# Attention scores of a unit's first query tile computed with the key tile stationary, copied out of PSUM and transposed back

## The reference, cut to what matters

```python
xn = layernorm(x)                                  # x: 2 x 512 x 512, f32
q = rope((xn @ wq).reshape(B, S, 32, 128))         # 32 query heads
k = rope((xn @ wk).reshape(B, S, 8, 128))          # 8 key heads, 4 query heads share one
v = (xn @ wv).reshape(B, S, 8, 128)
scores = einsum('bqhgd,bshd->bhgqs', qg, k) / sqrt(128)
allowed = (j <= i) & (j > i - 128)                 # causal, window of 128 keys
attn = softmax(where(allowed, scores, min))
s = einsum('bhgqs,bshd->bqhgd', attn, v) @ wo
g = silu(ffn(xn))                                  # 4-bit weights, dequantised
out = x + s * g
```

## Time and profile before

| | before |
|---|---|
| median of 3 runs | 899.94 us (899.69 to 900.66) |
| the profiled execution: its own time | 900.3 us |
| its span, first to last instruction | 898.1 us |
| mean granted TensorE clock | 0.998 |
| TensorE busy | 876.7 us (98%), 4384 matrix multiplications |
| TensorE weight loads | 740.6 us (82%) |
| VectorE, ScalarE, GpSimd busy | 648.1, 454.7, 467.2 us |
| DMA | 61.42 MB, mean 68 GB/s |

### The profile page before, as it was taken

One profiled execution on the slowest core, in us unless ns is written; L12 is line 12 of the kernel. 1 busy time (PEld: TensorE's weight loads), 2 busy tenths in 40 slices (PEclk: granted clock), 3 DMA queues, 4 the chain that ended last, 5 costly groups with the idle time before them and its releaser, 6 DMA issues. The chain is left out here.

```text
span 898.1 us, 14371 instructions
## 1 busy us (share of the span) xinstructions
PE 876.7 (98%) x4384; PEld 740.6 (82%) x4384; DVE 648.1 (72%) x1059; ACT 454.7 (51%) x1249; POOL 467.2 (52%) x363
## 2 busy tenths in 40 slices
PE   5989999999999999999999999999999999999997
PEld 4878888888888888888888888888778888888885
DVE  6787877877786877778687787778665567666556
ACT  4666555565656565565656556565652222213223
POOL 4674555555555545555455545654346435435435
PEclk9999999999999999999999999999999999999999
DMA  8021010111101111001101100003225365445452
GB/s 256 5 68 36 24 48 24 36 36 28 42 23 35 29 41 35 23 25 45 35 23 47 35 23 23 23 25 81 71 71 167 94 161 167 117 136 175 120 185 93
DMA packets 84442, 61.42 MB, mean 68 GB/s; under 512 B 3648, under 2 KB 71616, under 8 KB 84416
## 3 DMA queue, kind: packets, MB, share of 16 engines
q1 hardware_dynamic: 83696, 59.98, 23.1%
q10 hardware_dynamic: 720, 1.11, 0.3%
HBM read 58.98 MB, written 2.10 MB: 68 GB/s over the span
## 5 line engine op out<-in xcount | busy, mean ns | idle before, releaser
L36 PE MATMUL ps<-xt_hi,w_lo 128*128 128x512 f32 x604 | 236.8, 392 | 0.7 <-PEq L390 0.5
L37 PE MATMUL ps<-xt_lo,w_hi 128*128 128x512 f32 x604 | 235.6, 390 | 0.0
L38 PE MATMUL ps<-xt_hi,w_hi 128*128 128x512 f32 x604 | 235.1, 389 | 0.0
L853 POOL TENSOR_TENSOR q_lo<-work,q_hi 128x512 fp32r<-128x512 f32 x64 | 82.8, 1294 | 158.7 <-ACT q_hi L727 158.7
L858 POOL TENSOR_TENSOR pt_lo<-kept,pt_hi 128x512 fp32r<-128x512 f32 x112 | 143.7, 1301 | 29.4 <-ACT pt_hi L748 29.4
L38 PEld LDWEIGHTS ps<-xt_hi,w_hi 128*128 128x128 f32 x604 | 113.4, 188 | 23.9
L36 PEld LDWEIGHTS ps<-xt_hi,w_lo 128*128 128x128 f32 x604 | 113.6, 188 | 23.1 <-issue 0.9
L37 PEld LDWEIGHTS ps<-xt_lo,w_hi 128*128 128x128 f32 x604 | 113.7, 188 | 21.3
L737 ACT ACTIVATE probs<-ps,neg_max 128x128 f32<-128x128 f32 x256 | 90.7, 366 | 53.1 <-DVE neg_max L991 53.1
L748 ACT ACTIVATE pt_hi<-kept 128x512 fp32r<-128x512 f32 x112 | 69.2, 633 | 66.5 <-DVE kept L1001 66.5
L36 PE MATMUL ps<-wo_hi,o_lo 128*128 (+1 forms) x256 | 99.8, 390 | 0.1
(11 more groups left out here) (93 smaller groups left out, 1729.7 us busy)
## 6 DMA issues: line engine op xcount, KB each, us to landing
work<-L_attn_wq SPq DMA_DIRECT2D x32, 256.0 KB, 2.8
work<-L_attn_wo SPq DMA_DIRECT2D x32, 256.0 KB, 2.6
work<-L_ffn_gate_w SPq DMA_DIRECT2D x14, 256.0 KB, 3.3
work<-L_ffn_gate_z SPq DMA_DIRECT2D x14, 256.0 KB, 3.9
work<-L_ffn_gate_s SPq DMA_DIRECT2D x14, 256.0 KB, 5.3
work<-L_ffn_up_w SPq DMA_DIRECT2D x14, 256.0 KB, 3.3
work<-L_ffn_up_z SPq DMA_DIRECT2D x14, 256.0 KB, 4.0
work<-L_ffn_up_s SPq DMA_DIRECT2D x14, 256.0 KB, 4.4
```

The costliest lines, as they stand in the source:

```text
L36: pe.matmul(out, stat[1], mov[0], start=first, stop=False)
L37: pe.matmul(out, stat[0], mov[1], start=False, stop=False)
L38: return pe.matmul(out, stat[0], mov[0], start=False, stop=last)
L853: pool.tensor_tensor(lo, row_of(unit, b, i), hi.bitcast(F32), ALU.subtract).then_inc(rope_split, 1)
```

## The change

Three things change, all at the step `j == 3` of the 15 units that have a unit behind them.

- `scores` for that first tile is replaced by `scores_by_key`: the key tile stands, and the queries of all four heads move at once, 3 matrix multiplications of 512 columns into the PSUM bank `by_key`. Keys are now on the partitions.
- ScalarE copies that bank to SBUF (`by_key_copy`, into `v_t`, which is free there), placed ahead of `hi_of_probs`.
- TensorE turns the copy head by head with four transposes (`turn_scores`) into the places where `scores` used to write. The projection that follows is cut in two: its first two k-tiles (6 matrix multiplications) go between `scores_by_key` and `turn_scores`, the other 6 behind. At g == 7, b == 0 there is no such projection, and nothing stands between.

`scores_ready`, for which VectorE waits, is now raised by the last of the four transposes.

```diff
+        by_key = ps[:, 4, :]
+        by_key_sb = v_t[:, :]
...
-            def project(g, unit, b, k):
-                wait(pe, w_split, g * NPIECE + (k + 1))
-                wait(pe, proj_drained, unit * PROJ + (k - 2 if k >= 3 else FREE[b][k]))
-                for t in range(KT):
+            def project(g, unit, b, k, ts=range(KT)):
+                if ts[0] == 0:
+                    wait(pe, w_split, g * NPIECE + (k + 1))
+                    wait(pe, proj_drained, unit * PROJ + (k - 2 if k >= 3 else FREE[b][k]))
+                for t in ts:
...
-                last.then_inc(proj_ready, 1)
+                if ts[-1] == KT - 1:
+                    last.then_inc(proj_ready, 1)
...
+            def scores_by_key(un, bn):
+                pe.wait_ge(exp_done, un * (QB * GQ))
+                pe.wait_ge(rope_split, un * 5 + 5)
+                k = [t[:, bn, 0:P] for t in (k_hi, k_lo)]
+                q = [t[:, bn, :, 0:P] for t in (q_hi, q_lo)]
+                three_passes(pe, by_key, k, q, True, True).then_inc(by_key_ready, 1)
+
+            def turn_scores(un):
+                pe.wait_ge(by_key_out, un)
+                for h in range(GQ):
+                    last = pe.transpose(ps_score[:, h, 1, :], by_key_sb[:, h * P:(h + 1) * P], ident[:, :])
+                last.then_inc(scores_ready, 1)
...
                         turn_probs(n)
-                        if ahead and j == QB - 1:
-                            turn_v(un, bn)
                         if j < QB - 1:
                             scores(n + 1, unit, b, j + 1)
                         elif ahead:
-                            scores(n + 1, un, bn, 0)
+                            turn_v(un, bn)
+                            scores_by_key(un, bn)
+                            if not last:
+                                project(g + 1, unit + 2, b, 0, range(2))
+                            turn_scores(un)
                         if ahead and j < QB - 1:
                             project(gn, un, bn, before(g, b, j))
                         elif not last:
-                            project(g + 1, unit + 2, b, 0)
+                            project(g + 1, unit + 2, b, 0, range(2, KT))
...
+            def by_key_copy(un):
+                act.wait_ge(by_key_ready, un)
+                act.activation(by_key_sb, by_key, ACT.Copy).then_inc(by_key_out, 1)
...
                         more = ahead or j < QB - 1
+                        if ahead and j == QB - 1:
+                            by_key_copy(un)
                         hi_of_probs(unit, j)
```

More of the change, by code:

```diff
@@ L463, in attention_block @@
         o_hi_done = sem("o_hi_done")
+        by_key_ready = sem("by_key_ready")
+        by_key_out = sem("by_key_out")
         o_split = sem("o_split")
```

## The result

| | before | after |
|---|---|---|
| median | 899.7 us (8 runs) | 903.23 us (8 runs, 902.63 to 906.45) |
| ratio | | 1.0038, 95% interval 1.0025 to 1.0051 |
| profiled execution: own time, span | 900.3, 898.1 us | 903.18, 901.0 us |
| matrix multiplications | 4384 | 4309 in the records |

The account below looks back on a forecast made before the run. TensorE, never idle in the 14 inner units, was taken as the bound. Seven b == 0 transitions (2.59), seven b == 1 (-0.63) and the last (+0.43) gave +2.4 us, against the median 902.3 us; range 900.0 to 904.6.

Parts of the forecast that it names:

- TensorE alone gains 0.22 us per unit: TensorE at j == 3, first by_key multiplication to project_out: 3.93 to 3.94 us instead of 4.16.
- The copy costs nothing: ScalarE's copy ends at 1.55 us, before TensorE reaches the transposes at 2.13, covered by six projection multiplications.
- D = 0.93: Delay of VectorE's maximum at j == 3, from 153.72 to 154.65 us, passed on whole to both chains.
- Second chain, +0.37 seven times: GpSimd's pt_lo for the next unit's first tile, b == 0: second weigh_values multiplication starts 0.37 us later than before.
- First chain, -0.09: Through ScalarE's normalise: the multiplication behind the turned probabilities starts 0.09 us earlier, after a 0.13 us wait, all 14 inner units.
- g == 7: +0.43: Last unit, b == 0: no projection covers the copy and TensorE already waits, so all the delay shows, +0.43 us.
- The signs: TensorE idle some 0.1 us before probabilities' transposes, some 0.4 before L36 seven times; units of 40.24 and 39.78 us.
- The chains with more room: Rival: D about 0.75, so gain and waits cancel, +0.2, 900.1 us; chance 0.28.
- the faster one: Rival: no chain comes late, TensorE's 0.22 x 14 less 0.43 is gained, -2.7, 897.3 us; chance 0.08.
- the loads as the pace: Rival: weight loads pace TensorE, 12 to 7 per unit, time falls 12.7 us to 887.2 us; chance 0.02.
- The rooms: Time each chain has before TensorE would wait: 1.02 us for probabilities, 0.56 us for pt_lo at b == 0.

Follow-up runs that it names:

- e2: Changed kernel with v_hi (ScalarE) and v_lo (VectorE) moved out of the chain behind the scores into the idle time ahead of it: 897.12 us, ratio 0.9975.
- f1: Changed kernel with one k-tile of the projection (3 multiplications) ahead of turn_scores instead of two: 900.4 us, ratio 1.0002.
- f3: Changed kernel with ScalarE's copy placed behind hi_of_probs instead of ahead of it: 919.49 us, ratio 1.0209.
- e1: Changed kernel with GpSimd's two w_lo parts of b == 0, j == 3 put behind the next unit's first pt_lo: 900.32 us, ratio 1.0007.

## Why the prediction was right, and where it was off

The forecast was 902.3 us, +2.4; measured +3.5. By its own steps:

- *TensorE alone gains 0.22 us per unit.* It gains 0.18 (155.61 - 151.63 = 3.98 against 3.94). The instructions behind the first one after transposes are a few hundredths slow as well. The units of e2, where nothing waits, are 0.15 to 0.18 shorter than before.
- *The copy costs nothing.* Right; f1 and f3 show what it costs when its cover is cut or its place is moved.
- *D = 0.93.* It is 0.96.
- *Second chain, +0.37 seven times.* +0.39 at the instruction, and 40.31 - 39.87 = 0.44 over the unit (the seven such units average +0.41), 0.3 us more in all. Named with its place, its engine and its queue; e1 took it away by itself. At b == 1 about 0.9 us of room is left (206.43 to 207.78 is 1.35, against 0.45 where TensorE waits), the forecast said 1.0.
- *First chain, -0.09.* This is the term that was mis-sized. Six of the seven b == 1 units take 39.91 to 39.93 us, that is **+0.04**, and the last takes 39.81. The room of 1.02 us was worked out with 0.16 us from the end of `normalise` to the instruction behind the transposes, read in g == 7. In the loop it is 160.24 - 160.00 = 0.24. Of the 0.13 that were missed, 0.08 are this, 0.03 are D, and the rest are hundredths that the next instructions lose behind the wait. Over the seven units it is 0.8 us, most of the 1.2 us that the forecast was short in the trace (2.4 against 3.55). The forecast's range held it all the same.
- *g == 7: +0.43.* +0.49.
- *The signs.* The forecast looked for idle time of some 0.1 and 0.4 us on TensorE. Its rows show none at the first place and 0.12 us in the unit at the second (40.31 - 40.19), because rows overlap; the lengths of the units, forecast at 40.24 and 39.78, were the sign that could be read.
- *The rivals.* The chains with more room (0.28), the faster one, the loads as the pace: none came true. The busy time of the weight loads fell by 5.4 us, not by the 12.7 that the mean load gave, and the time rose by 3.5; in e2, where the full gain is had, 2.6 us come of 6.9 us less loading (740.6 to 733.7). The Trainium skill judges TensorE's headroom by this busy share, beside the share of the peak arithmetic rate (Perfetto Trace Analysis, Identifying the Most-Contended Engine). Read as a forecast of the time, it points the wrong way for this change.

The rooms were the right thing to read: 1.02 and 0.56 us. They stood in no view. By its busy time a unit with rooms of half a microsecond (39.87 of 39.87 us before) can't be told from one in which TensorE waits (39.92 of 39.92 in the changed kernel).

## What to carry to other kernels

On an engine that is never idle, an edit that saves its time can still lose if it makes a signal later. Before pricing the saving, follow the chain from the moved signal over every engine back to the busy one, and note the room at each place where it comes back, also behind the first (here the second, tighter room stood behind a key and two weights in GpSimd's queue). The repair is not to give up the saving but to shorten the chain by work that has no business in it: `v_hi` and `v_lo` sat between the exponentials and the reciprocals only by their order in the queue. With them moved, a change that cost 3.5 us became one that gains 2.6.

## What the runs showed of the hardware

When the transposes of probabilities have waited, TensorE goes on about 0.1 us later in the loop than in written-out code. In the changed kernel the distance from the end of `normalise` to the instruction behind the four transposes is 0.15 us in g == 0 (79.79 to 79.94) and g == 7 (601.28 to 601.43), and 0.24 to 0.26 in the loop (120.08 to 120.34, 160.00 to 160.24):

```profile
79.50 0.67 PE L628 MATMUL ps<-ident_sb,probs 128*128 128x128 f32 x4
79.94 0.35 PE L36 MATMUL ps<-k_hi,q_lo 128*128 128x256 f32 x1
```

```profile
119.78 0.68 PE L628 MATMUL ps<-ident_sb,probs 128*128 128x128 f32 x4
120.34 0.38 PE L36 MATMUL ps<-k_hi,q_lo 128*128 128x256 f32 x1
```

When TensorE doesn't wait there, the place costs the same in both (0.35 to 0.36 us from the first transpose to the scores, before). At the wait for `pt_lo` there is no such difference either: the second multiplication starts 0.45 us after GpSimd's end in written-out code (87.17 to 87.62) and in the loop (167.37 to 167.82).

Between the transposes and the score multiplication stand two waits, for `exp_done` and `rope_split`. Their counts are constants in written-out code, and in the loop they are worked out from its register. That this makes the 0.1 us is inferred from the place; no run took it away, and the cause stays open. The effect itself also shows in the last b == 1 unit, whose wait falls into written-out code: 39.81 us against 39.91 in the loop, and in e1 39.80 against 39.92.
